# Residual of all but the last chunks on GpSimd in two instructions, in an attention block with adaptive RMS norm and a quaternion rotation

## The chip, the cores and the metric

The kernel runs on one core of a Trainium2 chip. The metric is the device time of one execution in microseconds; the median of several runs is compared. Engines are called as in the profile: PE is TensorE (PEld its weight loads), DVE is VectorE, ACT is ScalarE, POOL is GpSimd, SP is the queue from which the DMAs are issued.

## What is computed

For x of 8 batches, 512 positions and 512 features, 16 heads of 32:

```
q, k, v = x Wq^T, x Wk^T, x Wv^T
attn    = softmax(where(mask, -inf, q k^T / sqrt(32)))
out     = (attn v) Wo^T
xn      = out / sqrt(mean(out^2) + 1e-6) * rms_scale * (1 + sc) + shift
x       = x + xn
x       = x + rotation(x)      (two Hamilton products, each of four output parts of 128 a signed sum of four)
```

`sc` and `shift` come from the conditioning vector of the batch. The spectral gate is the same for all frequencies, so that the last step is one fixed set of 16 products of 128 features per row, held in `rot` (with the identity added).

## The kernel before

**Projections (0 to about 290 us).** `projections` makes q, k and v of all batches by three matmul passes each (high and low parts) and stores them to scratch in DRAM.

**Attention (about 290 to 874 us).** `attention` goes through 34 groups, `GROUPS`. A group v is four heads of one batch (a unit u, 32 in all) and, for groups 0 to 29, all four chunks of 128 rows: 16 tiles. The last two units are cut into halves of two chunks, so groups 30 to 33 have 8 tiles each. Every engine has its own loop over the tiles n of `ORDER`, with the place t of a tile within its group, and what an engine does beside the tile's own work is hung on t by tables: `MASKS`, `EXPS`, `RESCALE`, `RESIDUAL`, `SQUARE`, `NORM_AT`, `PROJECT_AT`. The order of each engine is thus written out by hand, and semaphores tie them.

A tile: PE makes the scores (L108), DVE adds the mask and takes the row minimum (L117), ACT takes the exponential and its sum (L125), PE transposes the tile (L685), and DVE or ACT in turn move the transposed tile out of PSUM (L775, L876). At t = 1 of the next group PE multiplies with the values (L714) and transposes the inverse denominators (`turn_scale`, L695); these were spread over 32 columns by POOL (`spread_inverse`, L955) for groups up to 28, by ACT later. ACT moves them out, DVE multiplies (`norm`, L785), and the result is split into high and low part by POOL (`split`, L964, L966), or by ACT and DVE from group 29 on.

**The chunks.** Chunk m is 128 rows of the output; chunks 0 to 28 go the way told here, the last three (`LATE`) another one after the loop. In groups of m + 4 PE multiplies with Wo (L731) into PSUM. In group m + 5:

- ACT squares and sums it (`square`), POOL makes mean and 1/rms of the row in `rms(m)` (L983, L988), signalled by `rstd_ready`.
- DVE multiplies by rms_scale times (1 + sc) into the single buffer `scaled` (`rescale(m)`, L801).
- `residual(m)` on DVE (L808): x = scaled * rstd + x in one scalar_tensor_tensor, with x (and shift) in `x_of(m)`; it counts `summed`. Its place is t = 1 for m < 26 and t = 3 for chunks 26 and 27; for 28 t = 6 of group 33.
- POOL runs `rotate(m)`: 2048 products (L590), then two additions (L1009, L1011), which count `rotated`. Then `shift` of a later chunk adds the shift to its x (L977), counted by `shifted`.

POOL's order within a group v is set by its own loop:

```
if 0 < v <= POOL_GROUPS: spread_inverse(v - 1)
if v > NG: rms(v - NG - 1)
if 0 < v <= POOL_GROUPS: split(v - 1)
rotate(v - NG - 1); shift(v - NG)            # v <= 29
for m in LATE_SHIFTS[v]: shift(m)            # v >= 30,
rotate(v - NG - 1)                           # before the rotation
```

In group 30 `LATE_SHIFTS` is chunk 26, in 31 chunks 27 and 28, in 32 chunks 29 and 30, in 33 chunk 31. The x of chunks below 28 has two buffers in turn, and SP's `load_x` for chunk m waits for `rotated` of chunk m - 2. SP goes through the groups too: `load_x` (L634), `store` of a rotated chunk (L639), the q and k rows of a later unit (L74, L78), and in some groups the values or `load_mod` (L629), which waits for `summed`.

Of the kernel before, what the change touches and what calls it, by code (L numbers as in the profile page):

```python
# [5 lines left out]
ALU = mybir.AluOpType  # L6
# [14 lines left out]
NG = H // HG  # L21
# [9 lines left out]
V = len(GROUPS)  # L31
# [8 lines left out]
CHUNKS, LATE = TC * B - 3, (TC * B - 3, TC * B - 2, TC * B - 1)  # L40
# [6 lines left out]
LATE_SHIFTS = {V - 4: (V - 4 - NG,), V - 3: (V - 3 - NG, LATE_X), V - 2: (LATE_X + 1, LATE_X + 2), V - 1: (LATE_X + 3,)}  # L47
SQUARE = {(m + NG + 1, 0): m for m in range(CHUNKS - 1)} | {(V - 1, 2): CHUNKS - 1}
RESCALE = {(m + NG + 1, 1): m for m in range(CHUNKS - 1)} | {(V - 1, 2): CHUNKS - 1}
RESIDUAL = {(m + NG + 1, 1 if m < CHUNKS - 3 else 3): m for m in range(CHUNKS - 1)} | {(V - 1, 6): CHUNKS - 1}  # L50
MASKED = 1e30
QSCALE = -float(D) ** -0.5
RMS_EPS, NORM_EPS = 1e-6, 1e-8
# [2 lines left out]
def f32(ap):  # L56

    return ap.bitcast(F32)
# [439 lines left out]
def attention(nc, held, block, banks, x, scr, rows, scores, late, late_x, done, mod_scr, out, rot, ident, wo_hi, wo_lo):  # L498
# [4 lines left out]
    with ExitStack() as ctx:  # L503
        def sb(name, shape, dt=F32):
            return ctx.enter_context(nc.sbuf_tensor(name, shape, dt))

        def sem(name):
            return held.enter_context(nc.semaphore(name))
# [17 lines left out]
        scaled = sb("scaled", [P, E])  # L526
# [3 lines left out]
        rstd = sb("rstd", [P, 2])  # L530
# [18 lines left out]
        mean_ready, rstd_ready = sem("mean_ready"), sem("rstd_ready")  # L549
        scaled_ready = sem("scaled_ready")  # L550
        shifted = sem("shifted")
        summed = sem("summed")
# [31 lines left out]
        def take_waits(eng):  # L584

            eng.sem_inc(passed, 1)

        def rotation_products(eng, to, chunk):

            return eng.tensor_tensor(to.rearrange("p j (i d) -> p j i d", i=4), rot[:, :, :, :],  # L590
                                     chunk.rearrange("p (j d) -> p j d", j=4).unsqueeze(2).to_broadcast([P, 4, 4, C]),
                                     ALU.mult)
# [5 lines left out]
        late_stored = [sem(f"late_stored{j}") for j in range(3)]  # L598
        late_squared, late_scaled, late_rstd_ready = sem("late_squared"), sem("late_scaled"), sem("late_rstd_ready")
        late_mean, late_summed, late_mixed = sem("late_mean"), sem("late_summed"), sem("late_mixed")  # L600
        late_paired, late_added, late_rotated = sem("late_paired"), sem("late_added"), sem("late_rotated")

        def x_of(m):

            return late_x[:, m % TC] if m >= LATE_X else x_s[:, m % 2]
# [155 lines left out]
        def _(dve):  # L761
# [32 lines left out]
            def rescale(m):  # L794
                b = m // TC
                if m % TC == 0:
                    dve.wait_ge(mod_in[b % 2], 16 * (b // 2 + 1))
                dve.wait_ge(squared, m + 1)
                if m > 0:
                    dve.wait_ge(summed, m)  # L800
                dve.tensor_tensor(scaled[:, :], y_of(m), mod[:, b % 2, E:], ALU.mult).then_inc(scaled_ready, 1)  # L801

            def residual(m):
                c = m % TC
                dve.wait_ge(scaled_ready, m + 1)
                dve.wait_ge(rstd_ready, m + 1)
                dve.wait_ge(shifted, m + 1)
                dve.scalar_tensor_tensor(x_of(m), scaled[:, :], rstd[:, c % 2:c % 2 + 1], x_of(m),  # L808
                                         ALU.mult, ALU.add).then_inc(summed, 1)

# [21 lines left out]
            for n, (v, u, i, c) in enumerate(ORDER):  # L832
                t = n - FIRST[v]
                if t == INVERT_AT[SIZE[v]] and v > 0:
                    invert(v - 1)
                for _ in range(MASKS[SIZE[v]][t]):
                    if EARLY_END <= masks < N:
                        scores.mask(dve, masks)
                    masks += 1
                if (v, t) in RESCALE:  # L840
                    rescale(RESCALE[v, t])
                if (v, t) in RESIDUAL:
                    residual(RESIDUAL[v, t])
                if t == NORM_AT[SIZE[v]] and v > 0:
                    norm(v - 1)
                if t == LO_AT[SIZE[v]] and v > POOL_GROUPS:
                    split_lo(v - 1)
                if not by_act(n - 1) and n > 0:
                    move_out(n - 1)
# [99 lines left out]
        @block.gpsimd  # L949
        def _(pool):  # L950
            def spread_inverse(u):
                pool.wait_ge(inverted, u + 1)
                if u > 0:
                    pool.wait_ge(scale_turned, u)
                pool.tensor_copy(inv_d[:, :, :, :], inv[:, :, :].rearrange("p i c -> p c i").unsqueeze(3)  # L955
                                 .to_broadcast([P, TC, HG, D])).then_inc(spread, 1)

            def split(u):
                b, g = u // NG, u % NG
                if g == 0 and b >= 2:  # L960
                    pool.wait_ge(y_ready, TC * (b - 1))
                pool.wait_ge(normed, u + 1)
                take_waits(pool)
                pool.tensor_copy(o_hi[:, b % 2, g, :], o_T[:, :]).then_inc(o_hi_ready, 1)  # L964
                pool.wait_ge(o_hi_ready, u + 1)
                pool.tensor_tensor(o_lo[:, b % 2, g, :], o_T[:, :], f32(o_hi[:, b % 2, g, :]),  # L966
                                   ALU.subtract).then_inc(o_ready, 1)

            def shift(m):
                b, c = m // TC, m % TC  # L970
                if c == 0:
                    pool.wait_ge(mod_in[b % 2], 16 * (b // 2 + 1))
                if m >= LATE_X:
                    pool.wait_ge(late_in[c], 16)
                else:
                    pool.wait_ge(x_in[c % 2], 16 * (m // 2 + 1))
                pool.tensor_tensor(x_of(m), x_of(m), mod[:, b % 2, 0:E], ALU.add).then_inc(shifted, 1)  # L977

            def rms(m):
                c = m % TC  # L980
                pool.wait_ge(squared, m + 1)
                take_waits(pool)
                pool.tensor_scalar(mean_sq[:, c % 2:c % 2 + 1], sum_sq[:, c % 2:c % 2 + 1], 1.0 / E, RMS_EPS,  # L983
                                   ALU.mult, ALU.add).then_inc(mean_ready, 1)
                pool.wait_ge(mean_ready, m + 1)
                if m >= 2:
                    pool.wait_ge(summed, m - 1)
                pool.tensor_tensor(rstd[:, c % 2:c % 2 + 1], mean_sq[:, c % 2:c % 2 + 1], neg_half[:, :],  # L988
                                   ALU.pow).then_inc(rstd_ready, 1)

            def late_rms(j):
                to = late_rstd[:, j:j + 1]
                pool.wait_ge(late_squared, j + 1)
                pool.tensor_scalar(to, late_sum_sq[:, j:j + 1], 1.0 / E, RMS_EPS, ALU.mult, ALU.add).then_inc(late_mean, 1)
                pool.wait_ge(late_mean, j + 1)
                pool.tensor_tensor(to, to, neg_half[:, :], ALU.pow).then_inc(late_rstd_ready, 1)

            def rotate(m):
                c = m % TC
                pool.wait_ge(summed, m + 1)  # L1000
                if m >= 2:
                    pool.wait_ge(stored[c % 2], 16 * (m // 2))
                if m >= 1:
                    pool.wait_ge(rotated, m)
                rotation_products(pool, mix, x_of(m)).then_inc(mixing, 1)
                if m == CHUNKS - 1:
                    late_rms(0)
                pool.wait_ge(mixing, m + 1)
                pool.tensor_tensor(mix[:, 0:2, :], mix[:, 0:2, :], mix[:, 2:4, :], ALU.add).then_inc(paired, 1)  # L1009
                pool.wait_ge(paired, m + 1)  # L1010
                pool.tensor_tensor(acc[:, c % 2], mix[:, 0, :], mix[:, 1, :], ALU.add).then_inc(rotated, 1)  # L1011

            pool.wait_ge(turned, 1)
            pool.memset(neg_half[:, :], -0.5).then_inc(half_set, 1)  # L1014
            pool.wait_ge(half_set, 1)
            for v in range(V):
                if 0 < v <= POOL_GROUPS:
                    spread_inverse(v - 1)
                if v > NG:
                    rms(v - NG - 1)  # L1020
                if 0 < v <= POOL_GROUPS:
                    split(v - 1)
                if v <= POOL_GROUPS:
                    if v > NG:
                        rotate(v - NG - 1)
                    if v >= NG:
                        shift(v - NG)
                else:
                    for m in LATE_SHIFTS[v]:
                        shift(m)  # L1030
                    rotate(v - NG - 1)
            for j in (1, 2):
                late_rms(j)
# [69 lines left out]
```

## Time and profile before

| what | value |
|---|---|
| median of 3 runs | 875.37 us (875.3, 875.37, 876.35) |
| the profiled execution | 876.17 us, of which its span is 874.4 us |
| PE busy | 856.1 us, 98% |
| DVE busy | 628.4 us, 72% |
| ACT busy | 621.4 us, 71% |
| POOL busy | 481.7 us, 55% |
| granted TensorE clock | 0.999 of full speed (2.4 GHz) |
| chain that ended last | PE 95%, DVE 2%, the rest below 2% each |

The profile is of one execution. Busy shares are averages over two stages: in the first 290 us DVE, ACT and POOL have little to do. The chain that ended last is followed back from the last instruction to what released each step. Times in rows of the timeline count from the span's start; the bracket at the end of a row is the idle time of that engine before it, and what ended it.

### The profile page before, as it was taken

The page shows a single profiled execution, that of the slowest core. Times are in us where ns is not written, and L with a number is a line of the kernel's source. Part 1 is how long each engine was busy: PE and PEld are TensorE (multiplying, and loading weights), DVE is VectorE, ACT ScalarE, POOL GpSimd, SP SyncE. Part 2 cuts the span into 40 slices and gives each one's busy share as a digit, 9 for nine tenths or more (in the row PEclk, how much of TensorE's full clock was granted, in tenths as well). Part 3 has the DMA queues.
Part 4 walks back from the last instruction along what each step waited for, and adds up shares of the span by engine and source line. Part 5 has one row for each costly group of instructions (what it writes and reads, how often), then busy time and mean ns, then how long its engine had stood idle before and what let it go on. Part 6 is the DMA issues. An engine that isn't in the chain of part 4 may idle for free.

```text
span 874.4 us, 17160 instructions
## 1 busy us (share of the span) xinstructions
PE 856.1 (98%) x5334; PEld 638.5 (73%) x5334; DVE 628.4 (72%) x1516; ACT 621.4 (71%) x1505; POOL 481.7 (55%) x346
## 2 busy tenths in 40 slices
PE   6999999999999999999999999999999999999997
PEld 4878888888887665777677776777677776777674
DVE  4612212213316888999999999999999999999986
ACT  5322332332326889999999999999999999999882
POOL 0999990000000111277757776677757776677894
PEclk9999999999999999999999999999999999999999
DMA  8854554654596785577785778578766777669201
GB/s 273 333 180 182 208 191 178 212 191 173 175 296 228 164 192 116 134 196 161 157 207 127 165 183 207 121 170 208 156 169 170 161 163 197 155 144 233 83 26 49
DMA packets 82306, 153.75 MB, mean 176 GB/s; under 512 B 8472, under 2 KB 9112, under 8 KB 82224
## 3 DMA queue, kind: packets, MB, share of 16 engines
q1 hardware_dynamic: 82224, 152.75, 64.7%
q8 instruction: 40, 0.66, 0.3%
q14 instruction: 42, 0.34, 0.1%
HBM read 102.35 MB, written 50.36 MB: 175 GB/s over the span
## 4 chain that ended last, share of the span: by engine, by line
PE 95%; DVE 2%; issue 1%; DMA 1%; ACT 1%; SPq 0%; POOL 0%; DVEq 0%; ACTq 0%
PE banks L685 26%; PE banks L108 13%; PE banks L714 13%; PE banks L731 10%; PE banks L389 10%; PE banks L390 10%; PE banks L391 10%; PE banks L695 2%; DVE turned_probs L775 1%; DMA raw<-in_xT 1%; DVE probs L117 1%; DVE probs L590 0%; PE banks L425 0%; ACT turned_probs L876 0%; DVE banks L821 0%
## 5 line engine op out<-in xcount | busy, mean ns | idle before, releaser
L125 ACT ACTIVATE probs<-probs,least 128x512 f32<-128x512 f32 x512 | 363.4, 714 | 0.0
L117 DVE CUSTOM_DVE_ANT_0 probs<-banks,mask_bias 128x512 f32<-128x512 f32 x512 | 331.7, 680 | 31.4 <-PE banks L108 31.4
L685 PE MATMUL banks<-ident,probs 128*128 128x128 f32 x2048 | 308.6, 273 | 4.2 <-DVE turned_probs L775 1.9
L685 PEld LDWEIGHTS banks<-ident,probs 128*128 128x128 f32 x2048 | 245.5, 140 | 75.7 <-issue 15.9
L108 PE MATMUL banks<-k_rows,q_rows 128*128 128x512 f32 x496 | 236.2, 478 | 0.0
L775 DVE COPY turned_probs<-banks 128x512 f32<-128x512 f32 x256 | 175.6, 686 | 9.8 <-PE banks L685 9.7
L876 ACT ACTIVATE turned_probs<-banks 128x512 f32<-128x512 f32 x256 | 151.1, 590 | 34.8 <-PE banks L685 31.8
L328 DVE SCALAR_TENSOR_TENSOR late<-banks,late 128x512 fp32r<-128x512 f32 x64 | 44.1, 690 | 174.6 <-ACT late L294 174.6
L590 POOL TENSOR_TENSOR late<-rot,late 128x2048 f32<-128x2048 f32 x28 | 128.9, 4602 | 0.6 <-DVE late L808 0.6
L294 ACT ACTIVATE late<-banks 128x512 fp32r<-128x512 f32 x64 | 38.3, 598 | 120.1 <-PE banks L391 117.8
L714 PE MATMUL banks<-turned_probs,v_sb 128*32 128x512 f32 (+1 forms) x1088 | 116.9, 570 | 1.0 <-ACT turned_probs L876 1.0
L125 ACT ACTIVATION_READ_ACCUMULATOR probs<-probs,least 128x1 f32 x512 | 98.1, 192 | 0.0
L964 POOL CAST o_hi<-o_T 128x512 fp32r<-128x512 f32 x29 | 17.7, 611 | 144.4 <-DVE o_T L785 115.6
L108 PEld LDWEIGHTS banks<-k_rows,q_rows 128*128 128x128 f32 x496 | 94.2, 190 | 1.4
L1014 POOL MEMSET minus_half<- 128x1 f32 x1 | 0.1, 98 | 147.2 <-PE banks L685 147.2
L714 PEld LDWEIGHTS banks<-turned_probs,v_sb 128*32 128x32 f32 x1088 | 31.9, 109 | 62.8 <-issue 55.9
L1009 POOL TENSOR_TENSOR late<-late 128x1024 f32<-128x1024 f32 x29 | 69.5, 2397 | 2.2
L286 ACT ACTIVATE v_out<-banks 128x512 f32<-128x512 f32 x32 | 18.9, 597 | 63.4 <-PE banks L391 63.4
L389 PE MATMUL banks<-w_hi_v,x_hi 128*128 128x512 f32 x128 | 51.7, 404 | 7.5 <-DVE x_lo L342 7.5
L390 PE MATMUL banks<-w_lo_v,x_hi 128*128 128x512 f32 x128 | 51.2, 400 | 0.0
L391 PE MATMUL banks<-w_hi_v,x_lo 128*128 128x512 f32 x128 | 51.0, 399 | 0.0
L731 PE MATMUL banks<-wo_hi,o_hi 128*128 128x512 f32 x128 | 50.9, 397 | 0.0
(112 smaller groups left out, 1260.9 us busy)
## 6 DMA issues: line engine op xcount, KB each, us to landing
q_rows<-q_scratch SPq DMA_DIRECT2D x128, 256.0 KB, 6.0
k_rows<-k_scratch SPq DMA_DIRECT2D x124, 256.0 KB, 6.9
q_scratch<-late SPq DMA_DIRECT2D x64, 256.0 KB, 2.3
k_scratch<-late SPq DMA_DIRECT2D x64, 256.0 KB, 2.3
v_scratch<-v_out SPq DMA_DIRECT2D x32, 256.0 KB, 2.1
v_sb<-v_scratch SPq DMA_DIRECT2D x8, 1024.0 KB, 11.8
out<-late SPq DMA_DIRECT2D x29, 256.0 KB, 5.8
raw<-in_xT SPq DMA_DIRECT2D x7, 1024.0 KB, 5.7
```

Source lines behind the costliest of these rows:

```text
L108: pe.matmul(self.ps[:, n % 4, :], self.rows.q[:, u % 2, i, c * P:(c + 1) * P], self.rows.k_of(u)[:, i, :], start=True, stop=True).then_inc ...
L117: dve.tensor_tensor_reduce(self.probs[:, n % RING, :], self.ps[:, n % 4, :], self.mask_bias[:, c, :], 1.0, 3e38, ALU.add, ALU.min, self.le ...
L125: act.activation(self.probs[:, n % RING, :], self.probs[:, n % RING, :], ACT.Exp, bias=self.least[:, n % 32:n % 32 + 1], scale=-1.0, accum ...
L389: pe.matmul(out, hi(k), other_hi(k), start=(k == 0), stop=False)
L390: pe.matmul(out, hi(k), other_lo(k), start=False, stop=False)
L391: last = pe.matmul(out, lo(k), other_hi(k), start=False, stop=(k == KC - 1))
L590: return eng.tensor_tensor(to.rearrange("p j (i d) -> p j i d", i=4), rot[:, :, :, :], chunk.rearrange("p (j d) -> p j d", j=4).unsqueeze( ...
L685: last = pe.transpose(turn_ps[:, at % 2, j * P:(j + 1) * P], probs[:, n % RING, j * P:(j + 1) * P], ident[:, :])
L714: last = pe.matmul(value_ps[i * D:(i + 1) * D, cols], v_sb[:, b % 2, j, h * D:(h + 1) * D], turned_probs[:, (HG * u + i) % SLOTS, j, cols] ...
L731: last = pe.matmul(y_of(m), left[:, b % 2, k, t], right[:, k, :], start=(part == 0), stop=(part == 11))
L775: dve.tensor_copy(turned_probs[:, h % SLOTS, :, c * P:(c + 1) * P], turn_ps[:, PLACE["tile", n] % 2, :].rearrange("p (j t) -> p j t", j=TC ...
L876: act.activation(turned_probs[:, h % SLOTS, :, c * P:(c + 1) * P], turn_ps[:, PLACE["tile", n] % 2, :].rearrange("p (j t) -> p j t", j=TC) ...
```

## The change

For chunks 0 to 25 (`BY_POOL` = 26) the residual leaves DVE's order. `rotate(m)` on POOL starts with two new instructions in its place: a tensor_scalar that multiplies `scaled` by rstd in place (counting the new semaphore `normal`), and, after a wait for it, a tensor_tensor that adds it to x and counts `summed`. Chunks 26, 27 and 28 keep the residual on DVE, with one more wait, for `summed` of the chunk before.

```diff
-RESIDUAL = {(m + NG + 1, 1 if m < CHUNKS - 3 else 3): m for m in range(CHUNKS - 1)} | {(V - 1, 6): CHUNKS - 1}
+BY_POOL = CHUNKS - 3
+RESIDUAL = {(m + NG + 1, 3): m for m in range(BY_POOL, CHUNKS - 1)} | {(V - 1, 6): CHUNKS - 1}
...
+        normal = sem("normal")
...
                 dve.wait_ge(shifted, m + 1)
+                dve.wait_ge(summed, m)
                 dve.scalar_tensor_tensor(x_of(m), scaled[:, :], rstd[:, c % 2:c % 2 + 1], x_of(m),
                                          ALU.mult, ALU.add).then_inc(summed, 1)
...
             def rotate(m):
                 c = m % TC
+                if m < BY_POOL:
+                    pool.wait_ge(scaled_ready, m + 1)
+                    pool.wait_ge(rstd_ready, m + 1)
+                    pool.wait_ge(shifted, m + 1)
+                    pool.tensor_scalar(scaled[:, :], scaled[:, :], rstd[:, c % 2:c % 2 + 1], None,
+                                       ALU.mult).then_inc(normal, 1)
+                    pool.wait_ge(normal, m + 1)
+                    pool.tensor_tensor(x_of(m), scaled[:, :], x_of(m), ALU.add).then_inc(summed, 1)
                 pool.wait_ge(summed, m + 1)
```

POOL, from the split of group 28 (in group 29) to the shifts of group 31, as it was. The L590 rows are the rotations of chunks 24, 25 and 26; the L977 rows after the second L988 and the third are the shifts of chunk 26 and of chunks 27 and 28.

```order
L964 CAST o_hi<-o_T 128x512
L966 TENSOR_TENSOR o_lo<-o_T,o_hi 128x512
L590 TENSOR_TENSOR late<-rot,late 128x2048
L1009 TENSOR_TENSOR late<-late 128x1024
L1011 TENSOR_TENSOR late<-late 128x512
L977 TENSOR_TENSOR late<-late,mod_b 128x512
L983 TENSOR_SCALAR mean_sq<-sum_sq 128x1
L988 TENSOR_TENSOR rstd<-mean_sq,minus_half 128x1
L977 TENSOR_TENSOR late<-late,mod_b 128x512
L590 TENSOR_TENSOR late<-rot,late 128x2048
L1009 TENSOR_TENSOR late<-late 128x1024
L1011 TENSOR_TENSOR late<-late 128x512
```

The same stretch of POOL as it is now (L1007 and L1010 are the new instructions; line numbers have moved).

```order
L967 CAST o_hi<-o_T 128x512
L969 TENSOR_TENSOR o_lo<-o_T,o_hi 128x512
L1007 TENSOR_SCALAR scaled<-scaled,rstd 128x512
L1010 TENSOR_TENSOR late<-scaled,late 128x512
L591 TENSOR_TENSOR late<-rot,late 128x2048
L1020 TENSOR_TENSOR late<-late 128x1024
L1022 TENSOR_TENSOR late<-late 128x512
L980 TENSOR_TENSOR late<-late,mod_b 128x512
L986 TENSOR_SCALAR mean_sq<-sum_sq 128x1
L991 TENSOR_TENSOR rstd<-mean_sq,minus_half 128x1
L980 TENSOR_TENSOR late<-late,mod_b 128x512
L1007 TENSOR_SCALAR scaled<-scaled,rstd 128x512
```

Each rotation up to that of chunk 25 has two instructions more ahead of it, and nothing else has moved on POOL. From chunk 26 on its order is the old one.

DVE in group 32, as it is now (and as it was, but for line numbers): the place where the residual of chunk 27 (L811, before L808) still stands, ahead of the move L777 (before L775) of a transposed tile.

```order
L803 TENSOR_TENSOR scaled<-banks,mod_b 128x512
L777 COPY turned_probs<-banks 128x4x128
L118 ISA probs,least<-banks,mask_bias 128x512
L118 ISA least 128x1
L118 ISA probs,least<-banks,mask_bias 128x512
L118 ISA least 128x1
L118 ISA probs,least<-banks,mask_bias 128x512
L118 ISA least 128x1
L118 ISA probs,least<-banks,mask_bias 128x512
L118 ISA least 128x1
L811 SCALAR_TENSOR_TENSOR late<-scaled,rstd,late 128x512
L777 COPY turned_probs<-banks 128x4x128
```

In the full groups DVE's order has lost only the residual, between L801 and the next L775.

## Rows read from the trace of the kernel before

**Rows 1.** The page, busy time, share of the span and instructions.

```profile
PE 856.1 (98%) x5334; PEld 638.5 (73%) x5334; DVE 628.4 (72%) x1516; ACT 621.4 (71%) x1505; POOL 481.7 (55%) x346
```

**Rows 2.** Groups by form: line, engine, operation, shapes, count, busy us, mean ns, idle.

```profile
L808 DVE SCALAR_TENSOR_TENSOR late<-scaled,rstd,late 128x512 f32<-128x512 f32 x28 | 22.2, 792 | 0.9
...
L456 POOL TENSOR_SCALAR setup<-setup 128x256 f32<-128x256 f32 x1 | 0.4, 406 | 0.1
```

**Rows 3.** Timeline of POOL, one full group: start us, us, instruction [idle before].

```profile
512.84 0.61 POOL L964 CAST o_hi<-o_T 128x512 fp32r<-128x512 f32 x1 [4.79 <-issue]
513.53 1.30 POOL L966 TENSOR_TENSOR o_lo<-o_T,o_hi 128x512 fp32r<-128x512 f32 x1
514.78 4.61 POOL L590 TENSOR_TENSOR late<-rot,late 128x2048 f32<-128x2048 f32 x1
...
523.19 1.29 POOL L977 TENSOR_TENSOR late<-late,mod_b 128x512 f32<-128x512 f32 x1
524.42 0.62 POOL L955 COPY inv_d<-inv 128x512 f32<-128x512 f32 x1
```

**Rows 4.** Timeline of DVE at the start of the next full group.

```profile
523.20 0.69 DVE L775 COPY turned_probs<-banks 128x512 f32<-128x512 f32 x1
...
529.27 0.69 DVE L117 CUSTOM_DVE_ANT_0 probs<-banks,mask_bias 128x512 f32<-128x512 f32 x1 [0.85 <-PE banks L108]
```

**Rows 5.** Timeline of PE there.

```profile
523.59 0.47 PE L108 MATMUL banks<-k_rows,q_rows 128*128 128x512 f32 x1
524.04 0.63 PE L685 MATMUL banks<-ident,probs 128*128 128x128 f32 x4
...
528.17 0.66 PE L695 MATMUL banks<-ident,inv_d 128*128 128x128 f32 x4
528.58 0.48 PE L108 MATMUL banks<-k_rows,q_rows 128*128 128x512 f32 x1
528.90 0.60 PE L685 MATMUL banks<-ident,probs 128*128 128x128 f32 x4
```

**Rows 6.** Timeline of POOL from group 29's end to group 32.

```profile
808.32 1.29 POOL L1011 TENSOR_TENSOR late<-late 128x512 f32<-128x512 f32 x1
...
812.68 1.50 POOL L977 TENSOR_TENSOR late<-late,mod_b 128x512 f32<-128x512 f32 x1 [0.93 <-DMA late<-in_x]
814.12 4.61 POOL L590 TENSOR_TENSOR late<-rot,late 128x2048 f32<-128x2048 f32 x1
...
821.28 1.28 POOL L1011 TENSOR_TENSOR late<-late 128x512 f32<-128x512 f32 x1
...
825.55 1.30 POOL L977 TENSOR_TENSOR late<-late,mod_b 128x512 f32<-128x512 f32 x1 [1.52 <-DMA late<-in_x]
826.82 1.29 POOL L977 TENSOR_TENSOR late_x<-late_x,mod_b 128x512 f32<-128x512 f32 x1
828.75 4.61 POOL L590 TENSOR_TENSOR late<-rot,late 128x2048 f32<-128x2048 f32 x1 [0.63 <-DVE late L808]
...
837.53 0.55 POOL L988 TENSOR_TENSOR rstd<-mean_sq,minus_half 128x1 f32<-128x1 f32 x1
838.04 3.02 POOL L977 TENSOR_TENSOR late_x<-late_x,mod_b 128x512 f32<-128x512 f32 x2
```

**Rows 7.** Timeline of SP's queue: loads of the x of chunks 26 and 27.

```profile
809.63 0.33 SPq L634 DMA_DIRECT2D late<-in_x  x1
...
822.59 0.33 SPq L634 DMA_DIRECT2D late<-in_x  x1
```

**Rows 8.** Timeline of DVE: residuals of chunks 25, 26 and 27 (groups 30 to 32).

```profile
812.26 0.75 DVE L808 SCALAR_TENSOR_TENSOR late<-scaled,rstd,late 128x512 f32<-128x512 f32 x1
...
827.60 1.07 DVE L808 SCALAR_TENSOR_TENSOR late<-scaled,rstd,late 128x512 f32<-128x512 f32 x1
...
838.33 1.57 DVE L808 SCALAR_TENSOR_TENSOR late<-scaled,rstd,late 128x512 f32<-128x512 f32 x1
```

**Rows 9.** Timeline of PE in group 32.

```profile
840.65 0.63 PE L685 MATMUL banks<-ident,probs 128*128 128x128 f32 x4 [0.17 <-DVE turned_probs L775]
```

## The prediction

> **What bounds the kernel now.** The page's busy times come first: PE is busy 98% of the span, DVE 72%, POOL 55% [rows 1]. So an instruction taken from DVE is worth something only where PE waits for DVE, and one given to POOL costs something only where somebody waits for POOL. The averages don't say where that is; the timelines of a full group and of the last groups do.
>
> In a full group (17.9 us, as POOL's L590 repeats) PE runs without a stop but for one short delay at the group's start [rows 5], and POOL sits idle 4.8 us before the split, which waits for DVE's norm and through it for PE [rows 3]. In the last four groups, which have 8 tiles and last about half as long, POOL has the same rotation to do for each. There it has no such rest: it waits for a DMA, 0.9 and 1.5 us, and for DVE, 0.6 us, and for nothing else [rows 6]. The change must be judged at these two places apart.
>
> **Removed from DVE.** 26 residuals of 0.75 us (the 28 in rows 2 average 792 ns, the last two of them being drawn out [rows 8]): 19.5 us of DVE. I take the gain at zero. In a full group the residual lies between the rescale and a move, while PE is in its value matmuls, and right behind it DVE stands idle 0.85 us for PE's next scores [rows 4]. Without the residual that idle time becomes about 1.6 us, and from there on DVE is where it was. The bound on the gain is the delay of PE at the group's start, priced below as a rival.
>
> **Added to POOL.** Per chunk a tensor_scalar and a tensor_tensor of 128x512. The trace has no tensor_scalar of this size with a scalar per row. The nearest are the cast of one 128x512 input, 0.61 us [rows 3], and a tensor_scalar of half the length, 0.41 us [rows 2]; I take 0.61, as same size and one input. The upper bound is a two-input instruction, 1.30 us [rows 3]; the lower 0.41. The addition is two-input: 1.29. Each passes a semaphore that the next one waits for, which costs 0.08 us (the cast ends at 513.45, L966 starts at 513.53). So S = 0.69 + 1.37 = 2.06 us a chunk, between 1.86 and 2.75.
>
> **In full groups (chunks 0 to 24) it is hidden.** The two run after the split, so all from the rotation on is S later, up to the spread of the inverse denominators in the next group, and then POOL's 4.8 us of rest take it up; it does not add up from group to group. The spread now ends at 525.04 and PE's L695 that reads it starts at 528.17 [rows 3, 5]: 3.13 us of room, of which S takes 2.06 (2.75 at most). If it did not fit, PE would stall in each group. Nobody else feels it. The next rescale, which now waits for POOL's summed, comes some 9 us after it. SP's x load and store wait for the rotation and go out 2.06 us later; behind them SP waits for PE's scores of a tile in the middle of the group anyway, and the x is used by the shift of one group later. SP's load of mod waits for summed, which comes some 8 us later than on DVE (516.8 instead of 509.3 in the group of rows 3), but it stands behind the q and k rows, whose turn comes in the second half of the group, and behind it is only the next group's x load. The split itself stays on time. Cost zero.
>
> **At the end it is not hidden.** I follow the delay.
>
> 1. Group 29: the rotation of chunk 24 ended at 808.32 + 1.29 = 809.61 and is 2.06 late. SP issued the load of chunk 26's x at once, at 809.63, and POOL's shift of it waited for that load until 812.68 [rows 6, 7]. Load and shift are 2.06 later too: 814.74. The shift took 1.50 us, beside DVE's residual of 812.26 [rows 8]; that residual is gone, so 1.25 us to the next instruction in place of 1.44: 0.19 won.
> 2. Group 30: then chunk 25's own two instructions, another 2.06. L590 was at 814.12 and comes at 814.74 + 1.25 + 2.06 = 818.05, 3.93 late. Chunk 27's load goes out 3.93 late (822.59 becomes 826.52), and the shift that waits for it starts at 829.48.
> 3. Group 31: the shifts of chunks 27 and 28 took 2.56 us, to 828.11 [rows 6], now to 832.04. The rotation of chunk 26 then waited for DVE's residual until 828.75; that wait disappears, 0.63 won (the residual finds its rstd at about 827.4, just before DVE reaches it at 827.60, and isn't held). L590 starts at 832.0 instead of 828.75: 3.25 late.
> 4. Group 32: rstd of chunk 27 was ready at 837.53 + 0.55 = 838.08, and DVE took it up at 838.33 [rows 6, 8]. A quarter of a microsecond was all the room. Now it is ready at 841.33. DVE stands in front of its residual, and behind it in DVE's order is the move of a transposed tile for which PE already waited (840.65, released by L775 [rows 9]). PE stops.
>
> How long depends on one thing. The residual of 838.33 took 1.57 us instead of 0.75, beside two shifts on POOL. It ended at 839.90, which is 0.56 after the first of the shifts would be over (838.04 + 1.30). The one of 827.60 ended at 828.67, also 0.56 after the shift of 826.82 + 1.29 was over [rows 6, 8]. So its end hangs on POOL's shift and moves with it: shift 841.29, over at 842.59, residual over at 843.15, 3.25 late. Without this effect the residual would be over 0.75 after 841.38, 2.2 late. I take 3.25.
>
> The Trainium skill, SBUF — State Buffer (section on the two physically separate sides), says of the port pair that VectorE with two SBUF inputs shares with GpSimd that it is an exclusive lock, and the loser blocks until the other's instruction is over. By this rule the sum keeps 3.25, by additive costs it would be 2.2; the trace agrees, with its two ends 0.56 us after a shift.
>
> From there PE, DVE and POOL are all about 3.25 us late, and the rest of the program is waits among them and PE work that follows without gap. Nothing in it has spare time to give back. **Sum:** 2 x 2.06 - 0.19 - 0.63 - 0.05 (rounding of the starts) = 3.25 us. The profiled execution, 876.17 us with a span of 874.4, would be 879.4 with a span of 877.65. The median of the runs before is 0.8 below that execution, so the forecast is 875.37 + 3.25 = 878.6 us.
>
> **The rivals.**
>
> - **POOL becomes the bound in full groups.** If the scalar from a pointer makes the first instruction dear, S passes the 3.13 us of room, and each of the 24 full groups that follow a changed one grows by S - 3.13. If it cost what 1024 two-input elements cost here, 2.4 us, S is 3.85, and the loss 24 x 0.72 = 17 us, with 6.8 us at the end: about 899 us. Against it: the one-input cast and the short tensor_scalar are far below that.
> - **The relief of DVE reaches PE: faster.** At a group's start PE's transpose comes 0.45 us after the scores, at 524.04, where 0.32 is usual (528.58 to 528.90), and DVE's move of 523.20 is what frees its bank [rows 4, 5]. If DVE ran earlier everywhere, 0.13 us could be had in each of 25 full groups, 3.3 us, and if the end has more room than I see (DVE is also relieved in group 30), that remains: 872.1 us. It decides if DVE's backlog reaches over its waits for PE. Against it: DVE stands idle for PE right after the residual's place [rows 4], so what the residual costs it is gone before the next group's start.
> - **The delay at the end is absorbed.** If the load of x comes sooner after its issue (2.96 to 3.05 us now, in quiet queues), or if the residual of chunk 27 is not what PE needs, the loss falls below 1.75 us: 875.4 to 877.1. Against it is the 0.25 us of room only, and the wait of PE on L775 that is already there.
>
> **How the numbers follow.** My case, POOL late in the last groups, gets 0.74; the absorbed end 0.14; POOL bound in full groups 0.06; faster 0.06. A measurement can tell 0.2%, 1.75 us, from no change. Within my case the bounds of S give 2 x 1.86 - 0.87 = 2.85 and 2 x 2.75 - 0.87 = 4.63; with the unblocked residual 1.0 less at the low end. The median can itself lie 0.5 us off. So 877.2 to 880.0 for the case, and the range is drawn to 876.6 to 881.0, which takes in a part of the absorbed end. Slower: 0.74 + 0.06, less a little of my case that falls below 1.75 us: 0.79; same 0.15; faster 0.06.
>
> **What would show it.** In the profile after: the new tensor_scalar at about 0.61 us and the addition at 1.29; POOL's rest in a full group down from 4.8 to 2.7 us with the spread ending before 527.2 in the same group, and full groups still 17.9 us apart; DVE idle 1.6 us where it was 0.85; x loads of chunks 26 and 27 issued 2.1 and 3.9 us later; DVE waiting about 3 us for rstd in group 32 and PE about 3.4 us for L775's successor right after. I am wrong if full groups grow, or if group 32 shows no stall, or if the stall is there and the end gives it back.

## The result and the profile after

The changed kernel takes 882.57 us (median of 4 runs, 881.05 to 883.26), the kernel before beside it 875.51 us: a ratio of 1.0079, with a 95% interval of 1.0066 to 1.0091. It is slower by 7.06 us. The forecast was 878.6 us and the range ended at 881.0, so the prediction had the direction and was wrong on the size.

The page of the changed kernel, busy times as in [rows 1], and the chain that ended last:

```profile
PE 856.9 (97%) x5334; PEld 638.7 (73%) x5334; DVE 609.3 (69%) x1490; ACT 621.6 (71%) x1505; POOL 558.6 (64%) x398
...
PE 90%; POOL 4%; issue 2%; DVE 2%; DMA 1%; ACT 0%; SPq 0%; DVEq 0%; POOLq 0%
```

DVE has lost 19.1 us, as forecast. POOL has gained 76.9 us, where 26 chunks at 0.61 + 1.29 would have been 49.4. The groups by form (columns as in [rows 2]) show which of the two is dearer than thought:

```profile
L1007 POOL TENSOR_SCALAR scaled<-scaled,rstd 128x512 f32<-128x512 f32 x26 | 41.0, 1575 | 0.0
...
L1010 POOL TENSOR_TENSOR late<-scaled,late 128x512 f32<-128x512 f32 x26 | 33.6, 1294 | 2.2
```

The addition is at 1.29 us, the tensor_scalar at 1.58 instead of 0.61. The timeline of POOL in a full group, the counterpart of [rows 3]:

```profile
511.38 0.61 POOL L967 CAST o_hi<-o_T 128x512 fp32r<-128x512 f32 x1 [1.72 <-issue]
512.07 1.29 POOL L969 TENSOR_TENSOR o_lo<-o_T,o_hi 128x512 fp32r<-128x512 f32 x1
513.34 1.57 POOL L1007 TENSOR_SCALAR scaled<-scaled,rstd 128x512 f32<-128x512 f32 x1
515.00 1.29 POOL L1010 TENSOR_TENSOR late<-scaled,late 128x512 f32<-128x512 f32 x1
516.37 4.60 POOL L591 TENSOR_TENSOR late<-rot,late 128x2048 f32<-128x2048 f32 x1
...
524.76 1.30 POOL L980 TENSOR_TENSOR late<-late,mod_b 128x512 f32<-128x512 f32 x1
526.01 0.60 POOL L958 COPY inv_d<-inv 128x512 f32<-128x512 f32 x1
```

A chunk adds 516.37 - 513.34 = 3.03 us, not 2.06. POOL's rest ahead of the split is down from 4.8 to 1.7 us. PE and DVE at the same place (counterparts of [rows 5] and [rows 4]):

```profile
508.80 0.65 PE L697 MATMUL banks<-ident,inv_d 128*128 128x128 f32 x4
...
526.70 0.66 PE L697 MATMUL banks<-ident,inv_d 128*128 128x128 f32 x4
```

```profile
527.81 0.69 DVE L118 CUSTOM_DVE_ANT_0 probs<-banks,mask_bias 128x512 f32<-128x512 f32 x1 [1.64 <-PE banks L109]
```

PE still comes by every 17.90 us: the spread ends at 526.61 and PE reads it at 526.70, with 0.09 us to spare. DVE's relief of 0.75 us has become idle time, 1.64 us where it was 0.85. So the full groups cost nothing and gain nothing. The difference lies behind them. The last groups on POOL, then on DVE and PE (counterparts of [rows 6, 8, 9]):

```profile
814.08 1.28 POOL L980 TENSOR_TENSOR late<-late,mod_b 128x512 f32<-128x512 f32 x1 [0.70 <-DMA late<-in_x]
...
818.37 4.60 POOL L591 TENSOR_TENSOR late<-rot,late 128x2048 f32<-128x2048 f32 x1
...
829.64 1.29 POOL L980 TENSOR_TENSOR late<-late,mod_b 128x512 f32<-128x512 f32 x1 [1.92 <-DMA late<-in_x]
...
832.15 4.60 POOL L591 TENSOR_TENSOR late<-rot,late 128x2048 f32<-128x2048 f32 x1
...
840.96 0.55 POOL L991 TENSOR_TENSOR rstd<-mean_sq,minus_half 128x1 f32<-128x1 f32 x1
```

```profile
827.83 0.75 DVE L811 SCALAR_TENSOR_TENSOR late<-scaled,rstd,late 128x512 f32<-128x512 f32 x1 [0.82 <-issue]
...
841.62 1.67 DVE L811 SCALAR_TENSOR_TENSOR late<-scaled,rstd,late 128x512 f32<-128x512 f32 x1 [3.28 <-issue]
```

```profile
844.03 0.63 PE L687 MATMUL banks<-ident,probs 128*128 128x128 f32 x4 [3.64 <-DVE turned_probs L777]
```

The chain forecast is there: the loads are waited for, rstd of chunk 27 is late, DVE stands 3.3 us in front of its residual, PE 3.6 us behind DVE. One wait is there that the forecast had excluded. In group 31 DVE stood 0.82 us in front of the residual of chunk 26, whose rstd was ready only at 827.72 (827.15 + 0.57), and PE 0.49 us behind it:

```profile
829.33 0.63 PE L687 MATMUL banks<-ident,probs 128*128 128x128 f32 x4 [0.49 <-DVE turned_probs L777]
```

The page's slices don't show what comes next; the stretches of 2 us do (columns: length, then busy us of PE, PEld, DVE, ACT, POOL, then granted clock, DMA share, GB/s). First the changed kernel, then the one before:

```profile
842.00:844.00 2.00, 0.00 (x0) 0.00 (x0) 2.00 (x3) 0.00 (x0) 2.00 (x2) 1.00 0.08 30
844.00:846.00 2.00, 1.97 (x11) 1.70 (x12) 2.00 (x7) 0.93 (x3) 2.00 (x2) 0.78 0.00 0
846.00:848.00 2.00, 2.00 (x10) 1.75 (x9) 1.21 (x6) 0.75 (x3) 2.00 (x1) 0.50 0.00 0
848.00:850.00 2.00, 2.00 (x17) 1.51 (x20) 1.45 (x5) 1.56 (x4) 1.92 (x2) 0.87 0.00 0
```

```profile
844.00:846.00 2.00, 2.00 (x33) 1.25 (x35) 1.48 (x5) 2.00 (x7) 1.92 (x2) 1.00 0.03 8
846.00:848.00 2.00, 2.00 (x24) 1.31 (x16) 0.69 (x1) 2.00 (x7) 2.00 (x1) 1.00 0.00 0
```

After the stall the granted clock is at 0.5, 1.2 GHz, for some 3 us, and PE works at half speed. That costs 1.5 us more.

The first stage differs by a microsecond or two from execution to execution, so I count from PE's inverse transpose of group 29 (L695 before, L697 after), which lies 501.1 to 501.5 us behind the first one in all of the kernels in the table (501.12 before, 501.20 changed, and 501.46 in tail_only, where POOL has nothing more to do up to there: by this count too the full groups cost nothing). Times after that anchor, in us, each with its excess over the kernel before:

| kernel | anchor | PE goes on in group 32 | last value matmul | S |
|---|---|---|---|---|
| before | 796.67 | 43.98 | 57.04 | - |
| changed | 795.22 | 48.81 (+4.83) | 63.38 (+6.34) | 3.03 |
| ts2op | 795.74 | 47.21 (+3.23) | 61.87 (+4.83) | 2.16 |
| ttb | 796.19 | 48.27 (+4.29) | 62.68 (+5.64) | 2.50 |
| imm | 795.91 | 49.14 (+5.16) | 64.68 (+7.64) | 2.95 |
| tail_only | 795.92 | 48.98 (+5.00) | 62.03 (+4.99) | 3.03 |
| fill | 794.17 | 48.89 (+4.91) | 61.94 (+4.90) | 3.03 |
| by25 | 795.07 | 48.74 (+4.76) | 63.30 (+6.26) | 3.03, for chunk 24 but not 25 |
| ts_out | 796.21 | 49.82 (+5.84) | 64.38 (+7.34) | 3.03 |

The wait of 3.64 us is not the whole of the 4.83. PE came to group 32 already 1.37 us late (its inverse transpose there is at 836.07, 40.85 after the anchor, and was at 39.48), for the most part by the 0.49 us above and by 0.62 us for a load of q rows at 808.72. The latter comes and goes between executions: tail_only and fill don't have it and go on no earlier, since PE is late by what POOL is late.

### The profile page after: what moved, and what is told of

Read it like the earlier page. It is cut to its first block, busy times and chain, and to the rows that moved or that the text cites. A ratio compares the mean times of both kernels' runs of the same rounds, so it can differ in the third digit from the quotient of the medians.

```text
span 879.3 us, 17189 instructions
## 1 busy us (share of the span) xinstructions
PE 856.9 (97%) x5334; PEld 638.7 (73%) x5334; DVE 609.3 (69%) x1490; ACT 621.6 (71%) x1505; POOL 558.6 (64%) x398
## 4 chain that ended last, share of the span: by engine, by line
PE 90%; POOL 4%; issue 2%; DVE 2%; DMA 1%; ACT 0%; SPq 0%; DVEq 0%; POOLq 0%
PE banks L687 24%; PE banks L109 12%; PE banks L716 12%; PE banks L390 10%; PE banks L391 10%; PE banks L392 10%; PE banks L733 9%; PE banks L697 2%; POOL late L591 2%; POOL late L1020 1%; DVE turned_probs L777 1%; DMA raw<-in_xT 1%; POOL scaled L1007 0%; DVE probs L118 0%; POOL late L980 0%
## 5 line engine op out<-in xcount | busy, mean ns | idle before, releaser
L777 DVE COPY turned_probs<-banks 128x512 f32<-128x512 f32 x256 | 175.6, 686 | 11.4 <-PE banks L687 11.4
L733 PE MATMUL banks<-wo_hi,o_lo 128*128 128x512 f32 x128 | 51.1, 399 | 0.0
L733 PE MATMUL banks<-wo_lo,o_hi 128*128 128x512 f32 x128 | 51.0, 398 | 0.0
```

Of the source, the lines that this page charges most:

```text
L733: last = pe.matmul(y_of(m), left[:, b % 2, k, t], right[:, k, :], start=(part == 0), stop=(part == 11))
L777: dve.tensor_copy(turned_probs[:, h % SLOTS, :, c * P:(c + 1) * P], turn_ps[:, PLACE["tile", n] % 2, :].rearrange("p (j t) -> p j t", j=TC ...
```

## The experiments

The theory after the result (A): the loss is PE's stall in group 32, set by what POOL brings late into the half groups, about 2 S - 0.87 us, and the slow clock behind it. Open were why the tensor_scalar costs 1.58 us, whether full groups pay a share after all (C), and whether the part beyond the stall is the clock.

**imm: a constant in place of rstd.**

```diff
-                    pool.tensor_scalar(scaled[:, :], scaled[:, :], rstd[:, c % 2:c % 2 + 1], None,
+                    pool.tensor_scalar(scaled[:, :], scaled[:, :], 0.0442, None,
                                        ALU.mult).then_inc(normal, 1)
```

> As the changed kernel, but the new tensor_scalar on POOL multiplies by a constant instead of each row's rstd, so chunks 0 to 25 get a wrong norm. Theory A (the scalar read from a pointer makes the instruction dear): it takes about 0.62 us instead of 1.57, a chunk adds 2.06 us to POOL, and the end is late by 3.3 us: 878.8 us. Rival B (in-place writing or the port shared with VectorE makes it dear): it stays at 1.57 us and the time at 882.5.

883.31 us (ratio 1.0096, 1.0079 to 1.0112), and the instruction is hardly cheaper:

```profile
L1007 POOL TENSOR_SCALAR scaled<-scaled 128x512 f32<-128x512 f32 x26 | 39.1, 1503 | 2.2
```

The pointer accounts for 0.07 us. The explanation I had for the dear instruction falls. The executions took the time of rival B, but the run doesn't show B's cause.

**ttb: a tensor_tensor with rstd broadcast.**

```diff
-                    pool.tensor_scalar(scaled[:, :], scaled[:, :], rstd[:, c % 2:c % 2 + 1], None,
+                    pool.tensor_tensor(scaled[:, :], scaled[:, :], rstd[:, c % 2:c % 2 + 1].to_broadcast([P, E]),
                                        ALU.mult).then_inc(normal, 1)
```

> As the changed kernel, but the product with rstd is a tensor_tensor with rstd broadcast along the row; all results as before. Theory A: it costs as every two-input instruction of this size, 1.30 us, so 2.74 us a chunk; the end is late by 2 x 2.74 - 0.87 = 4.6 us plus up to 1.5 us of slower clock: 880 to 881.5 us. Rival B: 1.57 us or more, 882.5.

881.59 us (1.0071, 1.0054 to 1.0088).

```profile
L1007 POOL TENSOR_TENSOR scaled<-scaled,rstd 128x512 f32<-128x512 f32 x26 | 27.1, 1043 | 0.0
```

1.04 us, less than a tensor_tensor of two full inputs (1.30) and less than the tensor_scalar, with the same result. S is 2.50, and by 2 S - 0.87 PE should be 4.1 us late in group 32; it was 4.3, and the slow clock added 1.35.

**ts_out: not in place.** The tensor_scalar writes into the rotation's scratch, and the addition reads that.

```diff
+                    if m >= 1:
+                        pool.wait_ge(rotated, m)
-                    pool.tensor_scalar(scaled[:, :], scaled[:, :], rstd[:, c % 2:c % 2 + 1], None,
+                    pool.tensor_scalar(mix[:, 0, :], scaled[:, :], rstd[:, c % 2:c % 2 + 1], None,
...
-                    pool.tensor_tensor(x_of(m), scaled[:, :], x_of(m), ALU.add).then_inc(summed, 1)
+                    pool.tensor_tensor(x_of(m), mix[:, 0, :], x_of(m), ALU.add).then_inc(summed, 1)
```

> As the changed kernel, but the tensor_scalar writes to the rotation's scratch instead of in place, and the addition reads that. If writing in place is what makes it dear, it takes about 0.62 us; if not, 1.57 as before.

A single run, 883.05 us. It stays at 1.58 us, so writing in place is not it:

```profile
L1009 POOL TENSOR_SCALAR late<-scaled,rstd 128x512 f32<-128x512 f32 x26 | 41.0, 1579 | 0.0
```

PE goes on 0.65 us later than 2 S - 0.87 gives. Chunk 26's shift waited longer for its load here, issued at 812.21 and followed by the shift at 815.99, 3.8 us; in the changed kernel it was 2.9 (811.22 to 814.08). So the sum holds only to within what the loads of x vary.

**ts2op: two operations in the same instruction.** Every tensor_scalar that POOL runs in the kernel before has two.

```diff
-                    pool.tensor_scalar(scaled[:, :], scaled[:, :], rstd[:, c % 2:c % 2 + 1], None,
-                                       ALU.mult).then_inc(normal, 1)
+                    pool.tensor_scalar(scaled[:, :], scaled[:, :], rstd[:, c % 2:c % 2 + 1], 0.0,
+                                       ALU.mult, ALU.add).then_inc(normal, 1)
```

> As the changed kernel, but the tensor_scalar has two operations (times rstd, plus 0.0) like every tensor_scalar of the kernel before; the results are the same. Theory E (the form with a single operation is the dear one): it takes about 0.62 us, S is 2.06 us, and the forecast on record holds, 3.3 us later than before, 878.5 us. Rival F (any tensor_scalar of this length, or in this place, costs 1.5 us): 882.

879.93 us (1.0050, 1.0033 to 1.0067).

```profile
L1007 POOL TENSOR_SCALAR scaled<-scaled,rstd 128x512 f32<-128x512 f32 x26 | 18.1, 696 | 0.0
```

0.70 us. A useless "plus 0.0" makes the instruction more than twice as fast, and the change 2.6 us cheaper. The operands and the place in the order are those of the changed kernel, so neither they nor writing in place make the single operation dear, and rival B falls here. With S at 2.16, near the 2.06 of the forecast, PE is 3.23 us late in group 32, where the forecast said 3.25 and its sum with this S gives 3.45. The rest of the loss is again the clock, 1.6 us: so even with the right price the forecast of 878.6 is 1.3 us too low.

**fill: PE kept busy through the stall.** The added matmuls go into chunk 28's output.

```diff
+                if n == FIRST[V - 2] + 4:
+                    for _ in range(14):
+                        pe.matmul(y_ps, o_hi[:, 1, 0, 0:P], wo_hi[:, 0, :], start=False, stop=False)
                 turn(n)
```

> As the changed kernel, with 14 more matmuls of 128x512 on TensorE in group 32 right before the transpose that waits for VectorE, 3.3 us of work that takes the place of the idle time (they are added into chunk 28's output, which is wrong). Theory G (the loss beyond the stall is the granted clock, which fell to 0.5 after TensorE had stood for 3.6 us): the clock stays 1.0, and the time is 1.5 to 2.4 us below the changed kernel's, 880.2 to 881. Rival H (the time beyond the stall is lost otherwise): 882.5, or more by the added work.

880.36 us (1.0058, 1.0042 to 1.0075), 2.2 us less than the changed kernel although PE does 3.4 us more work. The interval overlaps with that of the changed kernel (1.0066 to 1.0091), so the traces have to decide. The transpose that was waited for, and the clock behind it:

```profile
843.06 0.63 PE L687 MATMUL banks<-ident,probs 128*128 128x128 f32 x4 [0.37 <-DVE turned_probs L780]
```

```profile
844.00:846.00 2.00, 2.00 (x16) 1.73 (x15) 2.00 (x6) 1.61 (x5) 2.00 (x1) 1.00 0.00 0
846.00:848.00 2.00, 2.00 (x27) 1.33 (x29) 1.89 (x7) 2.00 (x6) 2.00 (x1) 1.00 0.04 8
```

Counted from the anchor PE went on as late as in the changed kernel (+4.91 against +4.83), and from there to the last value matmul it took 13.05 us, as before, instead of 14.57. In the profiled execution the loss beyond the stall is the clock; theory G holds.

**by24: chunks 24 and 25 back on DVE.**

```diff
-BY_POOL = CHUNKS - 3
-RESIDUAL = {(m + NG + 1, 3): m for m in range(BY_POOL, CHUNKS - 1)} | {(V - 1, 6): CHUNKS - 1}
+BY_POOL = CHUNKS - 5
+RESIDUAL = {(m + NG + 1, {24: 4, 25: 1}.get(m, 3)): m for m in range(BY_POOL, CHUNKS - 1)} | {(V - 1, 6): CHUNKS - 1}
```

> As the changed kernel, but only chunks 0 to 23 on POOL; chunks 24 (place t = 4) and 25 (t = 1) are back on VectorE. Theory A (the whole loss arises in the last groups, where POOL has no rest): 875.5 us, no stall for rstd in group 32. Rival C (each full group pays a little, since the spread of the inverses now ends right before PE needs it): 24 of 26 parts of the loss stay, about 882.

876.44 us (10 runs; 1.0018, 1.0008 to 1.0027). This is 1.6 us more than before, where rival C expected 6.5 and I nothing. It doesn't lie in the full groups: from the first inverse transpose to the anchor they take 501.11 us, and took 501.12. Behind the anchor (796.16) PE waits for DVE once more in group 29, where the residual now stands at another place (at 802.00, 0.42 us), and for a load of q rows at 810.24 (0.34 us); the last value matmul is 1.07 us later than before. The rest of the 1.6 us was not traced.

**tail_only: chunks 24 and 25 alone on POOL.**

```diff
-RESIDUAL = {(m + NG + 1, 3): m for m in range(BY_POOL, CHUNKS - 1)} | {(V - 1, 6): CHUNKS - 1}
+RESIDUAL = {(m + NG + 1, 1 if m < 24 else 3): m for m in range(CHUNKS - 1) if m not in (24, 25)} | {(V - 1, 6): CHUNKS - 1}
...
-                if m < BY_POOL:
+                if m in (24, 25):
...
-                    pool.wait_ge(normal, m + 1)
+                    pool.wait_ge(normal, m - 23)
```

> As the kernel before, but chunks 24 and 25 alone have their residual on POOL; 0 to 23 stay on VectorE. Theory A (all of the loss comes from what enters the half groups late): the whole loss, 882 to 882.6 us. Rival C: 2 of 26 parts of it, 876.

882.49 us (1.0082, 1.0066 to 1.0099): two chunks make the whole loss. With by24 this settles where it arises, and C falls. The profiled execution was the fastest of the four (880.5 us), and in it the clock stayed at 1.0 behind a stall of 3.63 us (last value matmul +4.99); the others, up to 883.37, had a lower mean clock. So a stall of this length isn't always followed by the slow clock. That the others lost their time by it is likely from their mean clock, and no trace shows it.

**by25: only chunk 25 back on DVE, at t = 3.**

```diff
-BY_POOL = CHUNKS - 3
+BY_POOL = CHUNKS - 4
```

> As the changed kernel, but chunk 25's residual is back on VectorE (t = 3 of group 30), so POOL enters the half groups late by one chunk's 3.0 us instead of gaining a second one there. Theory A: the wait for rstd in group 32 is about 2 us instead of 3.3, PE's stall about 2.3 instead of 3.6, and no or less slow clock after it: 877.5 to 878.5 us. Rival C: about 882.

881.18 us (1.0053 to 1.0084), where 877.5 to 878.5 was expected. The dose was not what I meant it to be:

```profile
817.13 4.60 POOL L591 TENSOR_TENSOR late<-rot,late 128x2048 f32<-128x2048 f32 x1 [1.92 <-DVE late L811]
...
829.45 1.29 POOL L980 TENSOR_TENSOR late<-late,mod_b 128x512 f32<-128x512 f32 x1 [2.98 <-DMA late<-in_x]
```

POOL now waited 1.9 us for DVE's residual at its later place, and the x load of chunk 27, issued at 825.59, was there only 3.9 us later (2.8 in the changed kernel). Rotation 26 began 0.2 us earlier than in the changed kernel, and all the rest followed: PE stood 4.10 us in group 32, where about 2.3 was expected. So POOL is as late with one chunk's two instructions in the half groups as with two, and what it pays is not S alone. The run fits POOL's lateness as the cause, but it is no test of the size by dose.

**late27: DVE's residuals of chunks 26 and 27 behind the moves.**

```diff
-RESIDUAL = {(m + NG + 1, 3): m for m in range(BY_POOL, CHUNKS - 1)} | {(V - 1, 6): CHUNKS - 1}
+RESIDUAL = {(m + NG + 1, {26: 4, 27: 6}[m]): m for m in range(BY_POOL, CHUNKS - 1)} | {(V - 1, 6): CHUNKS - 1}
```

> As the changed kernel, but VectorE's residuals of chunks 26 and 27 stand later in their groups (t = 4 and 6 instead of 3), behind the moves that PE waits for. Theory A1 (PE's stall at that move is the loss): no stall over 1 us in group 32, granted clock 1.0 all through, below 878.5 us. Rival A2 (POOL's own lateness at the end is the bound wherever VectorE waits): the wait moves to a later place and 880 or more stays, less only what the slow clock cost, about 1.5 us.

881.51 us (1.0073, 1.0056 to 1.0090). PE passes the transpose, and stops 2.8 us at the next thing behind the residual, the low part of the values:

```profile
844.66 0.62 PE L733 MATMUL banks<-wo_hi,o_hi 128*128 128x512 f32 x1 [2.83 <-DVE o_lo L793]
```

The clock fell here too, to 0.5 between 846 and 848. A2 holds, with a gain of 1.1 us between the medians that is within their intervals: as long as DVE has to wait for a rstd that POOL makes late, its place changes little.

**no_res: no residual at all for chunks 0 to 25.**

```diff
                 if m < BY_POOL:
                     pool.wait_ge(scaled_ready, m + 1)
-                    pool.wait_ge(rstd_ready, m + 1)
...
-                    pool.tensor_tensor(x_of(m), scaled[:, :], x_of(m), ALU.add).then_inc(summed, 1)
+                    pool.sem_inc(summed, 1)
```

> Leaves out the residual of chunks 0 to 25 altogether: VectorE is relieved as in the change, POOL has no more than before (the rotation starts from x and shift alone). Theory A (relief of VectorE is worth nothing): 875.5 us within 0.5. Rival D (the relief reaches PE at the group starts): 872.

875.04 against 875.24 us (0.9997, 0.9988 to 1.0006; 11 and 15 runs). The relief of DVE is worth nothing here. As long as the orders of the engines otherwise stay as they are, this is also the bound for moving these 26 residuals off DVE: by the interval no more than 0.12% can be had.

**dummy: POOL's two instructions, but DVE keeps its residual.**

```diff
+                if m < CHUNKS - 3:
+                    pool.tensor_scalar(mix[:, 0, :], x_of(m), rstd[:, c % 2:c % 2 + 1], None,
+                                       ALU.mult).then_inc(normal, 1)
+                    pool.wait_ge(normal, 2 * m + 1)
+                    pool.tensor_tensor(mix[:, 0, :], mix[:, 0, :], x_of(m), ALU.add).then_inc(normal, 1)
+                    pool.wait_ge(normal, 2 * m + 2)
                 rotation_products(pool, mix, x_of(m)).then_inc(mixing, 1)
```

> The kernel before with two more instructions on POOL for each of chunks 0 to 25, of the same kind and size as the change's, on the rotation's own scratch (results not used); VectorE keeps its residual. Theory A (POOL's load alone makes the loss): 882 to 883 us, with the stall in group 32. If the semaphores moved to POOL or the relief of VectorE had a part in it, it lies 1 us or more away.

923.09 us (1.0547): a miss by 40 us, and instructive. In every full group DVE now waits for rstd, and PE for DVE:

```profile
522.05 0.75 DVE L809 SCALAR_TENSOR_TENSOR late<-scaled,rstd,late 128x512 f32<-128x512 f32 x1 [2.64 <-POOL rstd L989]
```

```profile
523.55 0.63 PE L686 MATMUL banks<-ident,probs 128*128 128x128 f32 x4 [1.51 <-DVE turned_probs L776]
```

Groups are 19.6 us apart (PE's L696 at 501.58, 521.14, 540.74) instead of 17.9. The cause is that rms(m) comes right behind the spread, so rstd too is late by S. It is the stall of group 32, in each group. The change escapes it in the full groups only because it moves the reader of rstd to POOL as well; where the reader stays on DVE (chunks 26 and 27), it strikes.

**edge: by24 with 0.69 us more on POOL.**

```diff
+                    pool.wait_ge(summed, m + 1)
+                    if m >= 1:
+                        pool.wait_ge(rotated, m)
+                    pool.tensor_copy(mix[:, 0, :], x_of(m)).then_inc(extra, 1)
+                    pool.wait_ge(extra, m + 1)
```

> As by24 (chunks 24 and 25 back on VectorE), with one more instruction on POOL for each of chunks 0 to 23: a copy of 128x512 into the rotation's scratch (not used), 0.69 us with its semaphore. That makes 3.71 us a chunk, 0.58 over the room of 3.13 us that the trace of before gave to the spread of the inverses. If that room is the bound, each of the 24 groups after a changed one grows from 17.9 to 18.5 us, 14 us in all, 890 us, and PE waits for the spread. If POOL's rest ahead of the split (4.8 us) is the bound instead, the time is by24's, 876.4.

891.74 us (2 runs; 1.0190, 1.0160 to 1.0219), 15.3 us above by24.

```profile
514.62 0.66 PE L698 MATMUL banks<-ident,inv_d 128*128 128x128 f32 x4 [0.58 <-POOL inv_d L959]
533.17 0.66 PE L698 MATMUL banks<-ident,inv_d 128*128 128x128 f32 x4 [0.58 <-POOL inv_d L959]
```

PE waits 0.58 us for the spread, the excess of 3.71 over 3.13, and groups are 18.55 us apart, 0.65 more than before; 24 of them give 15.6 us, a little more than the 14 expected. The room read from the trace of before was right to a tenth of a microsecond, and the changed kernel sits 0.1 us inside it.

## Why the prediction was wrong

- **Removed from DVE: zero.** Right. DVE idles 1.64 us in the old place, and no_res gives 0.9997.
- **Added to POOL: this is the step that failed.** "I take 0.61, as same size and one input ... The upper bound is a two-input instruction, 1.30 us" and "S = ... 2.06 us a chunk, between 1.86 and 2.75". The instruction took 1.58 and S was 3.03, outside both ends. The row nearest in kind, the tensor_scalar of half the length at 0.41 us [rows 2], differs in the one thing that counts: it has two operations. With the second operation present the price was 0.70, and the time, 879.93 us, lay within the range: it is this price that carried the change out of it. That a single-input instruction can't cost more than a two-input one was an assumption, not a bound.
- **In full groups: zero.** Right, and by luck near the edge: room 3.13, use 3.03. The time to the anchor (501.12 us before, 501.20 changed), by24 with tail_only, and edge bear it out. The rival that made POOL the bound in full groups had the mechanism and its threshold right, and didn't set in.
- **At the end.** The path was right, from the x loads over POOL's rotations and rstd of chunk 27 to DVE's residual and PE. Its step 3 says that the residual of chunk 26 isn't held; with the dearer S it was, 0.82 us, which the later stall swallowed. With the measured S the same sum gives 2 x 3.03 - 0.87 = 5.2 us; 4.83 was measured from the anchor, and 4.91 to 5.84 in other kernels with this S for both chunks. With a price near the assumed one (ts2op) 3.23 was measured against 3.25 forecast; that it agrees so well is in part luck, since the sum with the S of that run gives 3.45. That DVE's residual ends about 0.56 us after POOL's shift was read right too: the one of chunk 27 took 1.67 us, 841.62 to 843.29, beside shifts that began at 841.48, so it ended 0.51 us after the first of them would be over (841.48 + 1.30). The exclusive lock that the Trainium skill gives in SBUF — State Buffer (SBUF: two separate sides) fits: in the changed kernel the residual of chunk 26, at 827.83 with no shift beside it, took 0.75 us, where it was 1.07 before [rows 8].
- **"Nothing in it has spare time to give back."** True, but something took more: the clock. PE stood 3.6 us, and the granted clock went to 1.2 GHz for some 3 us: 1.5 us in the profiled execution of the changed kernel, 1.35 to 2.5 us in those of the others, 2.2 us between the medians of the changed kernel and fill. No term and no rival of mine had it. The Trainium skill, TensorE: Matmul & The Clock Gate (Why this matters for your kernels), warns that a gap in which TensorE idles between bursts of matmuls drops it to half rate. The runs here agree in most cases: stalls of 2.8 to 4.2 us were followed by it, that of 3.63 us in tail_only's profile was not.

The sum, mended: in the profiled execution 4.83 us of stall and 1.51 us of clock make 6.34 us. The medians are 7.06 us apart. The three executions without a profile had a mean clock of 0.996, the profiled one 0.998. imm's profiled execution, also at 0.996, had the slow clock for about 7 us and lost 2.5 us by it:

```profile
846.00:848.00 2.00, 2.00 (x8) 1.60 (x8) 1.63 (x4) 0.82 (x3) 2.00 (x1) 0.50 0.00 0
848.00:850.00 2.00, 2.00 (x10) 1.74 (x9) 0.83 (x3) 0.76 (x3) 1.95 (x1) 0.50 0.00 0
```

With 2.5 us in place of 1.5 the sum is 7.3 us. That this is what happened in the other executions of the changed kernel is an inference and not shown.

## What to carry to other kernels

A duration taken from a neighbouring row is only good for the same form of the instruction: on this engine the number of operations is part of the form (0.70 against 1.58 us), as is a broadcast operand (1.04 against 1.29), and "fewer operands" is no upper bound. When work moves to an engine with idle time, look for the values that this engine makes and others read (here rstd, with 0.25 us of room in one place of the program), and at the stretches where its work per group stays the same while the groups get shorter. A forecast stall of TensorE of the length seen here (2.8 to 4.2 us) needs a second term for the clock behind it, 1.35 to 2.5 us here, in all profiled executions but one.

## What the runs showed of the hardware

- GpSimd, 128x512 fp32: tensor_scalar with one operation 1.58 us with a scalar per row, 1.50 with a constant, in place or not; with two operations (times, plus 0.0) 0.70; tensor_tensor with one operand broadcast from a column 1.04; with two full operands 1.29; cast 0.61. What makes the single-operation form dear was not found.
- After PE had stood 2.8 to 4.2 us the granted clock was 0.5 for 3 to 4 us in the profiled executions of the changed kernel, ts2op, ttb, ts_out, by25 and late27, and for about 7 us in imm's (stall of 3.8 us). After 3.63 us in tail_only's it stayed at 1.0. With 3.4 us of matmuls in the gap (fill) it stayed at 1.0.
- A load of 128 rows of x was followed by the shift that waits for it 2.8 to 3.9 us after its issue, in the half groups of different kernels.
